# Moving row normalisation to GpSimd, the last value products past the batch boundary, and repeating narrow score products in a fused attention and expert kernel

## What is computed

```python
qkv = x @ qkv_w.T                          # 16 heads of 16
q, k = rotary(q), rotary(k)
outs = [sdpa(q[:, :6], k[:, :6], v[:, :6], 1 / sqrt(16)),          # dot heads
        hyp_attn(q[:, 6:10], k[:, 6:10], v[:, 6:10], curvature),   # softmax of 1/(eps + arccosh distance)
        sdpa(qn[:, 10:], kn[:, 10:], v[:, 10:], sqrt(16))]         # cosine heads
x = layernorm(x + concat(outs) @ proj_w.T + proj_b)                # all of them causal
x = layernorm(x + experts(x) + bias)       # the routing lists name rows of batch 0 only
```

## Time and profile before

| | us |
|---|---|
| median of 3 runs | 2299.3 (2297.95 to 2302.31) |
| the profiled execution | 2287.28 |
| its span, first to last instruction | 2285.4 |
| TensorE busy in the span | 1799.4 (79%) |
| ScalarE busy | 1417.4 (62%) |
| VectorE busy | 1355.4 (59%) |
| GpSimd busy | 714.8 (31%) |
| mean granted TensorE clock | 0.90 of full speed |

### The profile page before, as it was taken

The page is one execution under the profiler, slowest core; times in us unless marked ns, Lnnn a source line. Parts: engine busy times, 40 slices in busy tenths (PEclk is TensorE's granted clock), DMA queues, the critical chain, the costliest instruction groups (busy, mean ns, idle before and its releaser), DMA issues. The chain is left out here.

```text
span 2285.4 us, 40063 instructions
## 1 busy us (share of the span) xinstructions
PE 1799.4 (79%) x13330; PEld 960.5 (42%) x13330; DVE 1355.4 (59%) x3184; ACT 1417.4 (62%) x1400; POOL 714.8 (31%) x404
## 2 busy tenths in 40 slices
PE   6888888843887886896897797897788689646994
PEld 3344443421333443442443343443344344235894
DVE  4777676763654765765776585576576576550103
ACT  2333333322889887887888888888788788711110
POOL 0000000000434544544544544444454465520002
PEclk9999999976988997997998998998899799778997
DMA  5222233328044044125305405504404420109972
GB/s 192 89 106 107 110 111 111 111 100 167 11 76 67 11 67 116 26 38 105 66 8 96 105 2 94 106 10 85 113 11 68 111 51 25 52 35 353 352 277 67
DMA packets 88454, 217.45 MB, mean 95 GB/s; under 512 B 14112, under 2 KB 34848, under 8 KB 83936
## 3 DMA queue, kind: packets, MB, share of 16 engines
q1 hardware_dynamic: 79840, 184.74, 31.1%
q0 software_dynamic: 8448, 30.41, 4.2%
HBM read 146.52 MB, written 68.58 MB: 94 GB/s over the span
## 5 line engine op out<-in xcount | busy, mean ns | idle before, releaser
L1065 ACT ACTIVATE a_PT<-a_s 128x1024 f32<-128x1024 f32 (+3 forms) x576 | 459.6, 809 | 181.0 <-PE a_s L885 108.5
L882 PE MATMUL a_s<-a_Q,a_K 96*128 96x512 bf16 (+7 forms) x1152 | 335.7, 356 | 123.6 <-ACT a_PT L1065 78.0
L1261 DVE TENSOR_REDUCE a_mx<-a_w 128x1 f32<-128x512 f32 (+2 forms) x576 | 308.0, 551 | 55.3 <-PE a_w L910 42.3
L1143 POOL TENSOR_TENSOR a_Z<-a_Z,a_R 128x2182 f32<-128x2182 f32 x64 | 290.4, 4537 | 144.3 <-ACT a_R L1077 144.2
L897 PE MATMUL a_o<-a_PT,a_V 128*32 128x512 f32 (+3 forms) x2304 | 269.9, 543 | 77.8 <-ACT a_PT L1065 47.5
L1140 POOL TENSOR_TENSOR a_R<-a_Z 128x2182 f32<-128x2182 f32 x64 | 245.0, 3828 | 259.8 <-DVE a_Z L1253 196.7
L1253 DVE TENSOR_SCALAR_CACHE_REDUCE a_Z<-a_w 128x512 f32<-128x512 f32 (+7 forms) x384 | 202.6, 529 | 146.5 <-PE a_w L925 101.9
L245 PE MATMUL p_ps<-p_xT,p_w 128*128 128x512 f32 x512 | 243.6, 635 | 44.7 <-ACT p_xT L341 23.8
L942 PE MATMUL a_w<-a_ident,a_R 128*128 128x128 f32 (+1 forms) x1152 | 209.1, 309 | 24.9 <-POOL a_R L1150 13.8
L1307 DVE COPY a_PTh<-a_w 128x512 f32<-128x512 f32 (+1 forms) x256 | 157.7, 621 | 112.1 <-PE a_w L942 108.7
L910 PE MATMUL a_w<-a_K,a_Q 96*128 96x512 bf16 (+2 forms) x576 | 187.6, 333 | 34.5 <-DVE a_mx L1261 11.4
(11 more groups left out here) (161 smaller groups left out, 2799.7 us busy)
## 6 DMA issues: line engine op xcount, KB each, us to landing
e_w<-in_w SPq DMA_DIRECT2D x23, 2048.0 KB, 9.1
qk_parts<-p_parts SPq DMA_DIRECT2D x32, 768.0 KB, 3.5
a_Q<-qk_parts SPq DMA_DIRECT2D x144, 128.0 KB, 5.3
a_K<-qk_parts SPq DMA_DIRECT2D x144, 128.0 KB, 7.6
v_rows<-p_vt SPq DMA_DIRECT2D x8, 2048.0 KB, 7.7
a_V<-v_rows SPq DMA_DIRECT2D x32, 512.0 KB, 8.7
p_xin<-in_x SPq DMA_DIRECT2D x8, 1024.0 KB, 6.7
a_X<-in_x POOLq DMA_DIRECT2D x8, 1024.0 KB, 8.2
```

The source lines that it names most:

```text
L882: m = pe.matmul(sB[x % 2][:, i, 0:w], Kb[0:r, h, P * j:P * j + P], Qb[0:r, h, t0:t0 + w], start=True, stop=not diag)
L1065: act.activation(PT[:, u % 2, 2 * k:2 * k + 2, 0:w], sB[x % 2][:, :, 0:w], ACT.Exp, scale=scale_of(GROUPS[g][2 * k])).then_inc(prob.sem, 1)
L1143: pool.tensor_tensor(z, z, r, ALU.add).then_inc(z_sum.sem, 1)
L1261: dve.tensor_reduce(mx[:, pc, col:col + 1], wB[x % WB][:, 0:w], AX.X, ALU.max).then_inc(wide_free.sem, 1)
```

## The change

Five edits, all in `attend`:

1. GpSimd does `normalize`, in one item directly behind newton (slots 112 and 130). The addition of 1e-5 moves too: ScalarE takes the variance with a bias tile `tiny`, and newton gets a fifth small operation.
2. Values 35 and sums 5 go to slots 2 and 3 of the next batch's first step (after its second scores there); step 36 is gone.
3. Each score product of a narrow quad is issued HB // w more times with the same operands and the same target ahead of the real one: two more for w = 256, four more for w = 128.
4. Statistics 1 in four items of two (slots 122 to 125), variance 1 at 126, inverse_root 0 at 107, inverse_root 1 at 128, rows_out at 136 (behind square 7), rows_in at 143 (behind add_root 7).
5. turn_sums 5, 6 and 7 one slot later (150, 154, 158).

```diff
-        work = [[[] for _ in range(NSLOT)] for _ in range(NQ + 1)]
+        work = [[[] for _ in range(NSLOT)] for _ in range(NQ)]
...
-        for u in range(1, NQ + 1):
-            work[u][VALUES if u < NQ else 0].append(("values", u - 1))
-            if (u - 1) % 12 in (3, 11):
-                work[u][VALUES + 1 if u < NQ else 0].append(("sums", 2 * ((u - 1) // 12) + ((u - 1) % 12 == 11)))
...
+        for u in range(1, NQ + 1):
+            put(u * NSLOT + VALUES, ("values", u - 1))
+            if (u - 1) % 12 in (3, 11):
+                put(u * NSLOT + VALUES + 1, ("sums", 2 * ((u - 1) // 12) + ((u - 1) % 12 == 11)))
...
-        for at, item in ((25, ("shift",)), (104, ("variance", 0)), (106, ("inverse_root", 0)),
-                         (112, ("newton", 0)), (114, ("normalize", 0, 0)), (115, ("normalize", 0, 1)), (116, ("mid_out",)),
-                         (121, ("add_bias",)), (123, ("statistics", 1, 0, NT // 2)), (124, ("statistics", 1, NT // 2, NT)),
-                         (125, ("variance", 1)), (126, ("inverse_root", 1)), (129, ("newton", 1)),
-                         (131, ("normalize", 1, 0)), (132, ("normalize", 1, 1)), (133, ("rows_out",)), (141, ("rows_in",))):
+        for at, item in ((25, ("shift",)), (104, ("variance", 0)), (107, ("inverse_root", 0)), (112, ("newton", 0)),
+                         (112, ("normalize", 0)), (116, ("mid_out",)), (121, ("add_bias",)),
+                         (122, ("statistics", 1, 0, 2)), (123, ("statistics", 1, 2, 4)), (124, ("statistics", 1, 4, 6)),
+                         (125, ("statistics", 1, 6, 8)), (126, ("variance", 1)), (128, ("inverse_root", 1)),
+                         (130, ("newton", 1)), (130, ("normalize", 1)), (136, ("rows_out",)), (143, ("rows_in",))):
             put(at, item)
...
                     r = rows_of(h)
+                    for _ in range(HB // w if w <= HB // 2 else 0):
+
+                        pe.matmul(sB[x % 2][:, i, 0:w], Kb[0:r, h, P * j:P * j + P], Qb[0:r, h, t0:t0 + w],
+                                  start=True, stop=True)
                     m = pe.matmul(sB[x % 2][:, i, 0:w], Kb[0:r, h, P * j:P * j + P], Qb[0:r, h, t0:t0 + w],
...
-                act.wait_ge(var_ready.sem, var_ready.at(d, a))
-                act.activation(rs[:, 1], rs[:, 0], ACT.Ln).then_inc(rs_ln.sem, 1)
+                act.wait_ge(stats.sem, stats.at(d, 2 * NT * (a + 1) - 1))
+                act.activation(rs[:, 1], mv[:, :, 1], ACT.Ln, bias=tiny[:]).then_inc(rs_ln.sem, 1)
...
+                    hold(pool, rs_exp.sem, rs_exp.at(d, n), pool_passed)
+                    step(0, pool.tensor_scalar(rs[:, 0], mv[:, :, 1], 1e-5, None, ALU.add))
...
+                elif kind == "normalize":
+
+                    for t in range(NT):
+                        ins = pool.tensor_scalar(X[:, t, :], X[:, t, :], mv[:, t, 0:1], rs[:, 1, t:t + 1],
+                                                 ALU.subtract, ALU.mult)
+                    ins.then_inc(normed.sem, 1)
...
-                    dve.wait_ge(stats.sem, stats.at(d, 2 * NT * (a + 1) - 1))
-                    dve.tensor_scalar(rs[:, 0], mv[:, :, 1], 1e-5, None, ALU.add).then_inc(var_ready.sem, 1)
-                elif kind == "normalize":
-                    _, a, part = item
-                    if part == 0:
-                        dve.wait_ge(rs_step.sem, rs_step.at(d, 4 * a + 3))
-                    for n in range(NT // 2 * part, NT // 2 * (part + 1)):
-                        ins = dve.tensor_scalar(X[:, n, :], X[:, n, :], mv[:, n, 0:1], rs[:, 1, n:n + 1],
-                                                ALU.subtract, ALU.mult)
-                    if part:
-                        ins.then_inc(normed.sem, 1)
```

More of the change, by code:

```diff
@@ L682, in columns_of @@
             return hs[0] * NT, (hs[-1] + 1) * NT
-        SUMS = {0: 119, 1: 123, 2: 143, 5: 149, 6: 153, 7: 157, 3: 178, 4: 181}
+        SUMS = {0: 119, 1: 123, 2: 143, 5: 150, 6: 154, 7: 158, 3: 178, 4: 181}
         for n, at in SUMS.items():
@@ L719, in attend @@
             tail += [("turn_rows", n + 1)] * (n + 1 < NT) + [("project", n), ("statistics", 0, n, n + 1)]
-        tail += [("variance", 0), ("inverse_root", 0), ("newton", 0), ("normalize", 0, 0), ("normalize", 0, 1), ("mid_out",),
+        tail += [("variance", 0), ("inverse_root", 0), ("newton", 0), ("normalize", 0), ("mid_out",),
                  ("add_bias",), ("statistics", 1, 0, NT), ("variance", 1), ("inverse_root", 1), ("newton", 1),
-                 ("normalize", 1, 0), ("normalize", 1, 1), ("rows_out",)]
+                 ("normalize", 1), ("rows_out",)]
         tail_wide = {item: x for x, item in enumerate([it for it in tail if it[0] in RINGED])}
@@ L775, in attend @@
         rs = sb("a_rs", [P, 3, NT])
+        tiny = sb("a_tiny", [P, 1])
         first = sb("a_first", [P, C])
@@ L806, in attend @@
         y_inv, stats = ev("a_y_inv", NT), ev("a_stats", 4 * NT)
-        var_ready, rs_ln, rs_exp = ev("a_var", 2), ev("a_rs_ln", 2), ev("a_rs_exp", 2)
-        rs_step, normed = ev("a_rs_step", 8), ev("a_normed", 2)
+        rs_ln, rs_exp = ev("a_rs_ln", 2), ev("a_rs_exp", 2)
+        rs_step, normed = ev("a_rs_step", 10), ev("a_normed", 2)
         biased = ev("a_biased")
@@ L991, in do @@
                 if kind == "values":
-                    apply_values(b, item[1])
+                    apply_values(d, item[1])
                 elif kind == "argument":
@@ L1020, in turn @@
                     for k, slot in enumerate(step):
-                        if u < NQ:
-                            if k == 0 and u == 0:
-                                pe.wait_ge(qk_here[0].sem, qk_here[0].at(b))
-                            if k == 0 and u in (12, 24):
-                                here = m_here[u // 24]
-                                pe.wait_ge(here.sem, here.at(b))
-                            if k % 2 == 0:
-                                scores(b, u, k // 2)
+                        if k == 0 and u == 0:
+                            pe.wait_ge(qk_here[0].sem, qk_here[0].at(b))
+                        if k == 0 and u in (12, 24):
+                            here = m_here[u // 24]
+                            pe.wait_ge(here.sem, here.at(b))
+                        if k % 2 == 0:
+                            scores(b, u, k // 2)
                         for item in slot:
@@ L1105, in turn @@
                     for k, slot in enumerate(step):
-                        if u < NQ and k % 2 == 0:
+                        if k % 2 == 0:
                             exponentials(b, u, k // 2)
@@ L1156, in do @@
                 elif kind == "newton":
-                    pool.wait_ge(rs_exp.sem, rs_exp.at(d, n))
                     def step(k, ins):
                         ins.then_inc(rs_step.sem, 1)
-                        pool.wait_ge(rs_step.sem, rs_step.at(d, 4 * n + k))
-                    step(0, pool.tensor_tensor(rs[:, 2], rs[:, 0], rs[:, 1], ALU.mult))
-                    step(1, pool.tensor_tensor(rs[:, 2], rs[:, 2], rs[:, 1], ALU.mult))
-                    pool.sem_inc(pool_passed, 1)
-                    step(2, pool.tensor_scalar(rs[:, 2], rs[:, 2], -0.5, 1.5, ALU.mult, ALU.add))
-                    step(3, pool.tensor_tensor(rs[:, 1], rs[:, 1], rs[:, 2], ALU.mult))
-                    pool.sem_inc(pool_passed, 1)
+                        hold(pool, rs_step.sem, rs_step.at(d, 5 * n + k), pool_passed)
+                    hold(pool, rs_exp.sem, rs_exp.at(d, n), pool_passed)
+                    step(0, pool.tensor_scalar(rs[:, 0], mv[:, :, 1], 1e-5, None, ALU.add))
+                    step(1, pool.tensor_tensor(rs[:, 2], rs[:, 0], rs[:, 1], ALU.mult))
+                    step(2, pool.tensor_tensor(rs[:, 2], rs[:, 2], rs[:, 1], ALU.mult))
+                    step(3, pool.tensor_scalar(rs[:, 2], rs[:, 2], -0.5, 1.5, ALU.mult, ALU.add))
+                    step(4, pool.tensor_tensor(rs[:, 1], rs[:, 1], rs[:, 2], ALU.mult))
+                elif kind == "normalize":
[3 more added lines that the diff above has]
+                    ins.then_inc(normed.sem, 1)
                 elif kind == "shift":
@@ L1223, in _ @@
             dve.memset(Kb[KR:KR + 3, 0:N_DOT, :], 1.0).then_inc(setup, 1)
+            dve.memset(tiny[:], 1e-5)
             dve.memset(mx[:], -3.0e38).then_inc(setup, 1)
@@ L1402, in do @@
                 elif kind == "sums":
-                    copy_sums(b, item[1])
+                    copy_sums(d, item[1])
             def turn(b, first=False):
```

## The result

The changed kernel takes 2362.1 us (median of 4 runs, 2356.5 to 2375.9) against 2300.6 us of the kernel before: a ratio of 1.028, 95% interval 1.023 to 1.032. The forecast was 2258 us, with a range of 2236 to 2288. The profiled execution took 2362.8, with a span of 2361.2 (before 2285.4).

A forecast was written before the change was run, and what follows sets the result against it. Waits between ScalarE (busy 152.1 us) and TensorE (151.4) were taken to bound the 182 us batch. 54 won - 9 for repeats - 3 at the end = 42 us: 2287.3 to 2245, 2258 on the median's scale; range 2236 to 2288.

The forecast's parts named there:

- the price: One normalising operation on GpSimd: taken as 0.52 us, between 0.41 and 0.62; eight cost 4.2 us.
- The repeats: Narrow halves: repeated score products cost 0.45 us each, five halves on the path, 2.25 us a batch.
- the tail: After the last batch: two bare normalisations, 4.2 us each instead of 2.67, and a small step; 3 us lost.
- the cover of squares 6 and 7: GpSimd's longer queue would not delay ScalarE; for square 6 there were 2.8 us to spare.
- Part (a): Slots 112 to 120: ScalarE's 2.60 us of waits go, x_mid's earlier landing cancels later statistics; 2.4 us a batch won.
- part (b): Slots 130 to 138: ScalarE's whole wait of 2.38 us for square 7 goes.
- Part (c): Batch boundary: first scores come before the last exponential, log_sum 7 follows root 7 sooner; 2.95 us gained.
- by nothing that is waited for: Slots 136 to 143: rows_out behind square 7 delays the DMA by nothing waited for, except by rows_in.
- Steps 26 to 28: Extra products may keep the clock up: 1.15 us gained a batch, or 0.9 lost if it falls.
- GpSimd becomes the bound: Rival: an operation above 0.75 us delays squares 6 and 7; at 1.2 us the gain is gone; chance 0.03.
- The repeated products set the pace: Rival: all 24 narrow halves a batch on the path, 0.45 us each at full clock, giving 2334; chance 0.08.

The follow-up runs named there:

- experiment 6: The changed kernel with three instead of eight operations in each normalisation, the other five row tiles left unnormalised: 2297.2 us, ratio 1.000.
- experiment 7: The kernel of experiment 6 with x_mid issued one slot earlier, ahead of square 6: 2270.5 us, ratio 0.986.
- the fastest version: The changed kernel with both normalisations on VectorE ahead of the squares, x_mid ahead of square 6, repeats at steps 26 and 27 alone: 2227.8 us, ratio 0.970.
- experiment 3: The kernel before with the repeated score products alone added: 2322.1 us, ratio 1.0115.
- experiment 5: The kernel before with values 35 and sums 5 in the next batch's first step, rows_out at 136 and rows_in at 143: 2299.5 us, ratio 1.001.
- Experiment 4: The kernel before with only values 35 and sums 5 moved to the next batch's first step: 2299.8 us, ratio 1.001.
- experiment 1: The changed kernel with the normalising operations moved back from GpSimd to VectorE: 2304.7 us, ratio 1.004.
- experiment 2: The changed kernel without the repeated score products: 2336.1 us, ratio 1.018.

## Why the prediction was wrong

The runs take 92 of the 104 us between 2258 and 2362 apart: 65 for the price (after to experiment 6) and 27 for x_mid (6 to 7). The 12.5 us left at 2270.5 are a balance. The repeats cost 22.6 instead of 9, and the tail of experiment 7 is 10.8 longer than before instead of 3. That makes 21 us too few counted, so the rest of the sum must have brought some 9 us more than counted; where was not separated.

**The step that failed** is the price of one normalising operation. It was put at 0.52 us and measures 1.22. Its upper bound, 0.62 us, came from the square by the length of a row. The square is a tensor_tensor, and the argument was that one tensor input cannot cost more than two. Alone the operation takes 1.22 too; the tensor_tensor of 256 elements does take 0.61. The bound was exact for its own form and said nothing of the other. With it fell the cover of squares 6 and 7: the working had 2.8 us to spare for square 6 and 1.5 for square 7, and ScalarE waits 4.93 and 4.82 us for them. The one tensor_scalar at hand, eight elements in 0.19 us, gave a fixed part and no slope. The Trainium skill (GPSIMD Engine Reference, section "Engine selection") calls GpSimd roughly line rate with one input; the rows speak against it here: eight operations take 9.65 us on GpSimd and 2.67 on VectorE.

**Part (a)** said that x_mid leaves and lands 2 to 3 us earlier and that this cancels against the later statistics. That is the second failed step, and the table of experiment 7 shows it. In after x_mid leaves 5.2 us later, since the eight operations and square 6 both stand ahead of it in GpSimd's queue. At the price predicted (experiment 6) it leaves 0.8 us earlier, and step 28 itself comes 1.6 us earlier behind step 25, so the 2 to 3 us are there. But VectorE, free of the normalisation, is ready for add_bias 2.9 + 1.6 = 4.5 us earlier, so its wait grows from 3.7 to 5.7 us. The prediction followed x_mid to its landing and not to VectorE, on which clamps, statistics and copies stand behind add_bias. In experiment 6 steps 25 to 31 are 3.8 us shorter than before, as 2.4 + 1.15 had it; from there to the second exponential of step 34 1.1 us are lost, where part (b) counted 2.4 won.

**Parts (a) and (b)** together hold where price and x_mid are right. In experiment 7 (three operations) steps 25 to 31 are 2.7 us shorter than before and from step 31 to the second exponential of step 34 2.5, 5.2 in all, where 2.4 + 2.4 + 1.15 = 5.95 were counted.

**Part (c)**: the mechanism is there, log_sum 7 comes 4.9 us behind root 7 as worked out. In after the stretch from the second exponential of step 34 to step 4 has 29.2 us (before 28.0), with ScalarE's wait for square 7 in it; in experiment 7 it has 26.0, repeats included. That rows_out moves "by nothing that is waited for" was wrong for a VectorE that normalises: it had kept square 7 off the second normalisation. What the boundary alone is worth in the fastest version is less than predicted, 0.9 us, as far as it can be told.

**The repeats**: the count of halves on the path was five, and 22.6 us were measured where 9 were counted. The stretches of experiment 3 show 0.9 us at steps 9 to 12, as said, and as much again at steps 12 to 18, where ScalarE was taken to be behind. Steps 26 to 28 had a gain of 1.15 or a loss of 0.9 at even odds. Both occur: in steps 25 to 29 a batch has 17.4 us where the clock stays up and 19.9 where it falls in spite of the repeats, against 18.9 without them; in after five of eight batches are of the first kind, three of the second.

**The tail** is 20.9 us longer from the last exponential to the end, not 3. Two bare normalisations give 2 x (9.65 - 2.67) = 14. Most of the rest comes from rows_in behind add_root 7. The prediction said that this is not on the path, as `shift` stands 25 slots on; but in the tail `shift` is the first item. GpSimd there, in the kernel before and then in experiment 5:

```profile
1997.19 0.96 POOL L1127 DMA_DIRECT2D a_X<-in_x  x1 [1.89 <-DMA out<-a_X]
1999.77 4.80 POOL L1143 TENSOR_TENSOR a_Z<-a_Z,a_R 128x2182 f32<-128x2182 f32 x1 [1.62 <-ACT a_R L1077]
2004.54 4.51 POOL L1172 TENSOR_TENSOR a_X<-a_X,a_bias 128x2048 f32<-128x2048 f32 x1
```

```profile
2000.77 4.79 POOL L1144 TENSOR_TENSOR a_Z<-a_Z,a_R 128x2182 f32<-128x2182 f32 x1 [4.19 <-ACT a_R L1078]
2005.50 0.96 POOL L1128 DMA_DIRECT2D a_X<-in_x  x1
2011.80 4.48 POOL L1173 TENSOR_TENSOR a_X<-a_X,a_bias 128x2048 f32<-128x2048 f32 x1 [5.35 <-DMA a_X<-in_x]
```

GpSimd waits 5.35 us for x to land, and its masks, on which TensorE's last transposes wait, stand behind `shift`. From the last exponential on `shift` starts after 4.9 to 5.0 us in the kernels of before and of experiments 3 and 4, and after 11.1 to 11.5 in every kernel with rows_in at 143. Experiment 4 has no longer tail than before (0.2 us); experiment 5, which moves rows_out and rows_in besides, has one 6.2 us longer.

**The rivals.** "GpSimd becomes the bound" is what happened, at its place and by its mechanism, with a chance of 0.03 that rested wholly on the bound. It put "the gain is used up" at 1.2 us; at 1.22 the kernel is 62 us slower, since x_mid, most of the tail and the full cost of the repeats were not in it. "The repeated products set the pace" is refuted by experiments 1 and 2.

## What to carry to other kernels

A price taken from another form of instruction is no bound, not even from the form with more inputs: give it a wide range, or carry the case in which it is double as a real rival. Before work moves to another engine's queue, list all that stands behind it there, transfers too, and follow each to whoever waits in order for its landing, in the tail as well as in a steady batch. And an instruction that merely waits can keep two others apart: rows_out ahead of square 7 cost a wait of 2.4 us and kept a normalisation at 1.38 us that takes 4.88 beside the square.

## What the runs showed of the hardware

- On GpSimd a tensor_scalar of 128x256 fp32 takes 0.85 to 1.22 us by its operands, a tensor_tensor of the same size 0.61, with one tensor as both inputs or with a broadcast column as the second.
- Two instructions of VectorE and GpSimd can stand in each other's way; in the cases here the one that starts second waits until the first is done. VectorE's four normalising operations take 4.88 us instead of 1.38 beside a square of GpSimd. VectorE's addition of two tensors takes 6.6 to 6.9 us instead of 2.29 when it starts 0.03 to 0.31 us behind GpSimd's add_root; when it starts 0.78 us ahead, it takes 2.29 and add_root 6.20 instead of 4.84.
- In the same code the granted clock at step 27 is 1.00 in some batches and 0.50 in others, and steps 25 to 29 then take 17.4 or 19.9 us.
